# A key tile and a value tile of the self attention's latent made together in the two halves of TensorE's rows

## The chip, the cores and the metric

One core of a Trainium2 chip runs the whole kernel. The metric is the device time in microseconds (us) of one execution, as the median of several. The engines are TensorE (PE, with its weight loads as PEld), VectorE (DVE), ScalarE (ACT), GpSimd (POOL) and SyncE (SP), which issues most DMAs.

## The reference

Four sequences of 512 rows and 256 columns pass through two blocks: a cross attention on a context of 512 rows, and then a self attention whose keys and values come out of a latent of 64 columns each, followed by a gated layer of experts. Cut to what the change touches:

```python
q = (src @ Wq).reshape(Bb, Tt, H, DH).transpose(0, 2, 1, 3)
k = (src @ Wk_c @ Wk).reshape(Bb, Tt, H, DH).transpose(0, 2, 1, 3)   # latent 64, then 256
v = (src @ Wv_c @ Wv).reshape(Bb, Tt, H, DH).transpose(0, 2, 1, 3)   # latent 64, then 256
q = _apply_rope(q, sin, cos)
k = _apply_rope(k, sin, cos)
attn = jnp.einsum('bhqd,bhkd->bhqk', q, k) / np.sqrt(DH).astype(np.float32)
attn = jax.nn.softmax(attn, axis=-1)
sa = jnp.einsum('bhqk,bhkd->bhqd', attn, v)
```

## The kernel before

The attentions are eight instances, n = 0 to 7: four cross attentions (kind "c"), then four self attentions (kind "s"). Each has 16 heads in four quarters (groups) of four heads, and a quarter has 16 steps s, one for each of 4 key tiles and 4 heads, so that an instance has 64 steps. In each step TensorE makes the scores of one unit (L1695, 98 x 512, bf16) and ACT takes their exponential (L909). In each odd step TensorE also makes two more score tiles for the row maxima of a later quarter, 12 pairs ahead (max_pair, L1637), and DVE reduces the pair (row_max, L1156). In each fourth step comes the product of four probability tiles with the values (values, L1665: four heads side by side, 128 x 512 in f32, two passes each). At step 8 of a quarter the last quarter's heads are turned (L1651), at step AT_MAX its maxima (L1644); the turned maxima go by ACT (L802) and a DMA (L807) into the query stack.

While instance n runs, its successor m = n + 1 is prepared in stage tiles, that the lists CROSS_STEPS and SELF_STEPS put at steps of n (a negative step lies in n - 1). FA_STEPS does the same for the output projection of the last self attention. "tile" is TensorE's work, "empty" the copy of that tile out of its bank by DVE or ACT (OWNER). Of a self attention tiles 0 and 1 are transposes, 2 and 3 the two halves (even, odd) of the queries, 4 the latent (both halves of 64 in one tile cT), 5 and 6 the two halves of the keys (L1566: rows 0 to 63 of TensorE, 512 columns, f32) and 7 and 8 the values (L1571: rows 64 to 127, twice 256 columns). DVE empties tiles 2, 3, 5 and 6 by rotating them (L1088 to L1094, two instructions each), ACT the values (L856). Then "sum" adds the two products of a rotation on POOL (L651), "part0" and "part1" are copies to bf16 on ACT (L829, L833), "rest" and "part2" differences on POOL (L656, L661). Each part is written to scratch by SP (L525, L531) and read back as the stacks of the next instance (L546, L560), of which the first quarter is needed by the pair at step 41.

Scores, turned maxima and stage tiles share three banks in turn: the order of PE's work gives each its slot, and one may start when the work three slots earlier has been emptied. TensorE's order is fixed, so a tile that waits for its slot holds up all that follows. Row maxima have two double banks of their own, in which turned heads also take a place.

The four lines that matter most:

```python
                    f = t - 5
                    last = MM(o, fkv[0:DC, f * P:(f + 1) * P], cT[0:DC, 0, :], start=True, stop=True)
...
                        last = MM(o[:, j * D:(j + 1) * D], cT[DC:2 * DC, 0, tt * P:(tt + 1) * P], fkv[DC:2 * DC, :],
                                  start=True, stop=True)
```

Of the kernel before, what the change touches and what calls it, by code (L numbers as in the profile page):

```python
# [14 lines left out]
P = 128  # L15
HG = 4
# [5 lines left out]
LEAD = 12  # L22
FILL = 24
PROB_SLOTS = 3
AT_COPY, AT_HEADS, AT_MAX, AT_ROWS = 4, 8, 9, 11
SCORE_BANKS = [0, 1, 7]
END_BANKS = [0, 1, 7, 6, 2, 3, 4, 5]

# [7 lines left out]
def flamingo_block(nc, x, ctx_in, g_xattn, g_ffn, wq, bq, wk, bk, wv, bv,  # L36
                   f_wq, f_wkc, f_wvc, f_wk, f_wv, f_wo, f_in, f_out, f_w1, f_w2,
                   f_gg, f_ge, f_gb, f_eb, n1, n2, rope, out):
    B, L, D = x.shape
# [17 lines left out]
    DC = f_wkc.shape[1]  # L57
# [13 lines left out]
    INST = [("c", 0), ("c", 1), ("c", 2), ("c", 3), ("s", 0), ("s", 1), ("s", 2), ("s", 3)]  # L71
# [13 lines left out]
    def hook(n, step, *what):  # L85
        a = n * UNITS + step
        HOOKS.setdefault((a // UNITS, a // STEPS % NG, a % STEPS), []).append(what)

    CROSS_STEPS = [("stats", 0, -34), ("norm", 1, -20), ("norm", 0, -16), ("tile", 2, -12), ("empty", 2, -12), ("tile", 0, -11),
        ("empty", 0, -11), ("tile", 3, -10), ("empty", 3, -10), ("tile", 1, -6), ("empty", 1, -6), ("tile", 4, -5),  # L90
        ("empty", 4, -5), ("tile", 5, -5), ("empty", 5, -5), ("tile", 6, -4), ("empty", 6, -4), ("part0", 0, -3),
        ("part1", 0, 1), ("rest", 0, 1), ("empty", 8, 2), ("tile", 8, 2), ("part2", 0, 2), ("tile", 7, 3),
        ("empty", 7, 3), ("part0", 1, 3), ("rest", 1, 4), ("tile", 9, 5), ("empty", 9, 5), ("part1", 1, 7),
        ("part2", 1, 10)]
    SELF_STEPS = [("stats", 0, -28), ("norm", 0, -21), ("norm", 1, -20), ("tile", 0, -14), ("empty", 0, -14), ("tile", 1, -9),
        ("empty", 1, -8), ("tile", 4, -4), ("empty", 2, -3), ("empty", 4, -3), ("tile", 2, -3), ("tile", 3, -2),
        ("empty", 3, -2), ("tile", 5, -1), ("empty", 5, 0), ("sum", 0, 1), ("tile", 6, 2), ("empty", 6, 2),
        ("sum", 1, 2), ("tile", 7, 5), ("empty", 7, 5), ("part0", 0, 5), ("rest", 0, 5), ("tile", 8, 7),
        ("empty", 8, 7), ("rest", 1, 8), ("part2", 1, 8), ("part0", 1, 10), ("part1", 0, 14), ("part2", 0, 14),
        ("part1", 1, 16)]  # L100
    FA_STEPS = [("fatile", 0, 12), ("faempty", 0, 12), ("faempty", 1, 15), ("fatile", 1, 15), ("faempty", 2, 19), ("fatile", 2, 19),
        ("fatile", 3, 23), ("faempty", 3, 23), ("fastats", 0, 32), ("nf", 0, 43)]

    SELF_NO = {m: sum(k_ == "s" for k_, _ in INST[:m + 1]) for m in range(NI)}
    for n in range(1, NI):
        m = n + 1
        if m < NI:
            for what, i, step in (CROSS_STEPS if INST[m][0] == "c" else SELF_STEPS):
                hook(n, step, what, m, i)
        if INST[n - 1][0] == "s":  # L110
            for what, i, step in FA_STEPS:
                hook(n, step, what, INST[n - 1][1], i)


    BEGIN = [[2, 3, 6, 7, 0, 1, 4, 5, 8, 9], [2, 3, 6, 7, 8, 0, 1, 4, 5, 9]]

    def kind_of(stage, m):
        return "fa" if stage == "fa" else "b" if m == 0 else INST[m][0]
# [5 lines left out]
    SLOTS = []  # L124

    for m_ in range(2):
        SLOTS.extend(("proj", m_, t_) for t_ in BEGIN[m_])
    SLOTS.append(("turned", 0))
    for u_ in range(NI * UNITS):
        n_, g_, s_ = u_ // UNITS, u_ // STEPS % NG, u_ % STEPS  # L130
        SLOTS.append(("unit", u_))
        if s_ == AT_MAX and u_ // STEPS + 1 < GROUPS:
            SLOTS.append(("turned", u_ // STEPS + 1))
        for what_, m_, i_ in HOOKS.get((n_, g_, s_), []):
            if what_ in ("tile", "fatile"):
                SLOTS.append(("proj" if what_ == "tile" else "fa", m_, i_))
    STAGE = [key for key in SLOTS if key[0] in ("proj", "fa")]
    SLOTS = [key for key in SLOTS if key not in ASIDE]
    SLOT = {key: k for k, key in enumerate(SLOTS)}

    FILLED, EMPTIED, done = {}, {}, {"A": 0, "V": 0}
    EMPTYING = [("proj", m_, t_) for m_ in range(2) for t_ in BEGIN[m_]]
    for a_ in range(NI * UNITS):
# [2 lines left out]
                        if what_ in ("empty", "faempty"))  # L146
    for key in STAGE:
        FILLED[key] = len(FILLED) + 1
    for key in EMPTYING:
        who = OWNER[kind_of(key[0], key[1])][key[2]]  # L150
        done[who] += 1
        EMPTIED[key] = (who, done[who])
# [77 lines left out]
    with es:  # L230
# [9 lines left out]
        fkv = sb("fkv", [P, D], F32)  # L240
# [34 lines left out]
        cT = sb("cT", [P, CT, L], F32)  # L275
# [92 lines left out]
        s_tf = sem("stage_tile_full")  # L368
# [414 lines left out]
        def _(act):  # L783
# [94 lines left out]
            def begin_second():  # L878
                for t in BEGIN[1][:4] + BEGIN[1][5:9]:
                    if t == 6:  # L880
# [589 lines left out]
        def _(pe):  # L1470
            MM, TR = nc.tensor.matmul, nc.tensor.transpose
# [11 lines left out]
            def emptied(key):  # L1483

                if key[0] == "unit":
                    pe.wait_ge(s_exp, key[1] + 1)
                elif key[0] == "turned":
                    pe.wait_ge(s_mts, key[1] + 1)
                else:
                    who, count = EMPTIED[key]  # L1490
                    if count > waited[who]:
                        waited[who] = count
                        pe.wait_ge(s_ta if who == "A" else s_tv, count)

            def take(key):
                if key in ASIDE:
                    return slot_bank(key)
                k = slots[0]
                slots[0] += 1
                assert SLOTS[k] == key  # L1500
                if k >= 3:
                    emptied(SLOTS[k - 3])
                return slot_bank(key)
# [43 lines left out]
            def self_tile(m, t):  # L1547
                b = INST[m][1]
                o = take(("proj", m, t))
                if t < CT:  # L1550
                    if t == 0:
                        pe.wait_ge(s_set, 1)
                        pe.wait_ge(s_w, 16 * N_LARGE)
                        pe.wait_ge(s_src, 2 * (m + 1))
                    last = turn(o, src[b], t)
                elif t < 4:
                    emptied(("proj", m, 1))
                    f = t - 2
                    last = product(o, [(fq[:, c, f * P:(f + 1) * P], nT[:, c, :]) for c in range(CT)])
                elif t == 4:  # L1560
                    emptied(("proj", m, 1))
                    last = product(o, [(fkvc[:, c, :], nT[:, c, :]) for c in range(CT)])
                elif t < 7:
                    emptied(("proj", m, 4))
                    f = t - 5
                    last = MM(o, fkv[0:DC, f * P:(f + 1) * P], cT[0:DC, 0, :], start=True, stop=True)  # L1566
                else:
                    emptied(("proj", m, 4))
                    for j in range(2):
                        tt = 2 * (t - 7) + j  # L1570
                        last = MM(o[:, j * D:(j + 1) * D], cT[DC:2 * DC, 0, tt * P:(tt + 1) * P], fkv[DC:2 * DC, :],  # L1571
                                  start=True, stop=True)
                last.then_inc(s_tf, 1)

            def begin():
# [4 lines left out]
                pe.wait_ge(s_id, 4)  # L1580
                for t in BEGIN[0]:
                    if t == 6:
# [4 lines left out]
                    cross_tile(0, t)  # L1587
                for t in BEGIN[1][:5]:
                    cross_tile(1, t)
# [97 lines left out]
            for n in range(NI):  # L1687
                for g in range(NG):
                    gi = n * NG + g
                    for s in range(STEPS):  # L1690
                        u = gi * STEPS + s
                        kt, h = divmod(s, HG)
                        if s == 0:
                            pe.wait_ge(s_mrow, (gi + 1) * 16)
                        MM(take(("unit", u)), ks[:, g, h, kt * P:(kt + 1) * P], qs[:, g, h, :],  # L1695
                           start=True, stop=True).then_inc(s_sT, 1)
                        if u == 0:
                            max_pair(LEAD - 1)
                        q = u // 2 + LEAD
                        if s % 2 and q < N_PAIRS:  # L1700
                            max_pair(q)
                        if h == HG - 1 and (kt or gi):
                            values(*((gi, kt - 1) if kt else (gi - 1, TT - 1)))
                        if s == AT_HEADS and gi > 0:
                            turn_heads(gi - 1)
                        if s == AT_MAX and gi + 1 < GROUPS:
                            turn_max(gi + 1)
                        for what, m, i in HOOKS.get((n, g, s), []):
                            if what == "tile":
                                (cross_tile if INST[m][0] == "c" else self_tile)(m, i)  # L1710
                            elif what == "fatile":
                                self_output(m, i)
# [177 lines left out]
```

## Time and profile before

| what | value |
|---|---|
| median of 3 executions | 781.66 us (779.74 to 782.42) |
| the profiled execution | 780.02 us |
| its span, first to last instruction | 778.2 us |
| mean granted TensorE clock | 0.993 |
| busy: PE, DVE, ACT, POOL | 743.0, 514.7, 408.5, 217.9 us |

The steps of the eight instances take the span from 50 to 525 us; what follows is the layer of experts. The profile's busy time of PE counts matmuls with modelled ends. Times below are us from the start of the span. A row of the timeline has the start, the duration, the engine, the line, the operation, out<-in, the shapes and a count, and in brackets the idle time of the engine before it with what ended it; instructions that follow each other are merged into one row.

### The profile page before, as it was taken

To read this page: it belongs to the slowest core of one execution; us is meant where nothing else is said; L and a number is where in the kernel's file an instruction comes from. 1 tells how busy PE (TensorE), PEld (TensorE's weight loads), DVE (VectorE), ACT (ScalarE), POOL (GpSimd) and SP (SyncE) were. 2 spreads that over 40 slices of the span, in tenths; PEclk is the share of its full clock that TensorE was granted. 3 is DMA by queue.
4 is the path that set the end of the run, shared out by engine and by line. 5 is a ranking of instruction groups with operands and counts; after the bars stand their busy time and mean duration, and the time that the engine had idled before them with its cause. 6 is when DMAs were issued, how large, how long until landed. Compare 5 with 4: busy or idle time off the path is not lost.

```text
span 778.2 us, 10386 instructions
## 1 busy us (share of the span) xinstructions
PE 743.0 (95%) x3534; PEld 342.0 (44%) x3534; DVE 514.7 (66%) x777; ACT 408.5 (52%) x767; POOL 217.9 (28%) x326
## 2 busy tenths in 40 slices
PE   8879999999999999999999999999999999999995
PEld 5422343243233233233423432424644766458884
DVE  5679848847978878878797788762457222532765
ACT  4356867777767776875774867675211221222000
POOL 5232133223315415303321510010103721400444
PEclk9999999999999999999999999999999999999998
DMA  8783233315215414512421232006001564000011
GB/s 266 203 241 79 59 108 125 82 47 193 61 51 165 125 42 123 150 41 83 126 80 41 96 110 83 1 2 217 0 1 74 203 202 153 24 1 1 28 41 41
DMA packets 51892, 73.31 MB, mean 94 GB/s; under 512 B 7808, under 2 KB 42880, under 8 KB 51840
## 3 DMA queue, kind: packets, MB, share of 16 engines
q1 hardware_dynamic: 47248, 63.80, 28.1%
q0 software_dynamic: 2816, 8.46, 2.9%
q8 instruction: 29, 0.48, 0.3%
q10 hardware_dynamic: 1776, 0.40, 0.3%
q14 instruction: 23, 0.19, 0.1%
HBM read 45.04 MB, written 27.33 MB: 93 GB/s over the span
## 4 chain that ended last, share of the span: by engine, by line
PE 71%; DVE 14%; ACT 5%; issue 3%; DMA 3%; POOL 2%; SPq 0%; POOLq 0%; DVEq 0%; ACTq 0%
PE ps L1512 31%; PE ps L1665 12%; PE ps L1695 12%; PE ps L1637 11%; DVE negm L1156 7%; ACT hS L909 3%; PE ps L1507 2%; POOL scrf L744 2%; DVE bst L1034 2%; PE ps L1571 1%; PE ps L1651 1%; DMA rows<-in_L_xattn_wq_dram 1%; DMA w<-mTs 1%; DMA scrq<-mix 1%; PE ps L1566 1%
## 5 line engine op out<-in xcount | busy, mean ns | idle before, releaser
L1156 DVE TENSOR_REDUCE negm<-ps 128x2 f32<-128x1024 f32 x256 | 303.5, 1220 | 72.0 <-PE ps L1637 64.4
L909 ACT ACTIVATE hS<-ps 128x512 f32<-128x512 f32 x512 | 280.7, 604 | 116.6 <-PE ps L1695 114.7
L1695 PE MATMUL ps<-w 98*128 98x512 bf16 x512 | 170.1, 385 | 9.5 <-DMA w<-mTs 4.7
L1637 PE MATMUL ps<-w 96*128 96x512 bf16 x512 | 154.4, 383 | 7.8 <-DVE negm L1156 4.4
L1665 PE MATMUL ps<-hS,mix 128*17 128x512 f32 x1024 | 134.7, 598 | 0.2
L1695 PEld LDWEIGHTS ps<-w 98*128 98x128 bf16 x512 | 43.8, 97 | 161.5 <-ACT hS L909 76.6
L1637 PEld LDWEIGHTS ps<-w 96*128 96x128 bf16 x512 | 47.8, 98 | 60.4 <-DVE negm L1156 10.8
L1356 DVE SCALAR_TENSOR_TENSOR ctxs<-qk,ps 128x512 f32<-128x512 f32 x32 | 22.0, 687 | 72.0 <-ACT qk L945 71.0
L945 ACT ACTIVATE qk<-ps 128x512 f32<-128x512 f32 x32 | 19.1, 597 | 81.6 <-PE ps L1512 81.6
L1512 PE MATMUL ps<-w,hS 128*128 x256 | 55.6, 379 | 0.0
L1512 PEld LDWEIGHTS ps<-w,hS 128*128 128x128 f32 x256 | 48.6, 190 | 7.0 <-issue 0.5
L656 POOL TENSOR_TENSOR qk<-qk,mix 128x1024 f32<-128x1024 f32 x14 | 29.8, 2129 | 50.9 <-ACT mix L829 50.6
L633 POOL TENSOR_TENSOR mdif<-bst 128x4 f32<-128x4 f32 x12 | 2.5, 206 | 146.5 <-DVEq L996 146.5
L1665 PEld LDWEIGHTS ps<-hS,mix 128*17 128x17 f32 x1024 | 17.0, 95 | 53.9 <-ACT hS L909 29.4
L671 POOL TENSOR_SCALAR hS<-hS,tg 128x256 f32<-128x256 f32 x16 | 14.9, 930 | 92.0 <-DVEq L1182 92.0
L651 POOL TENSOR_TENSOR qk<-qk,hT 128x1024 f32<-128x1024 f32 x8 | 18.8, 2351 | 76.1 <-DVEq L996 76.1
L661 POOL TENSOR_TENSOR mix<-qk,mix 128x1024 bf16<-128x1024 f32 x14 | 29.9, 2133 | 26.6 <-ACT mix L833 25.5
L1512 PE MATMUL ps<-cT,fin 128*128 128x512 f32 x64 | 28.6, 595 | 0.3 <-ACT cT L938 0.3
L744 POOL DMA_INDIRECT scrf<-rows,place x16 | 15.7, 978 | 47.1 <-DVEq L996 42.5
L1359 DVE SCALAR_TENSOR_TENSOR hS<-ctxs,ps 128x512 f32<-128x512 f32 x32 | 22.0, 687 | 10.0 <-PE ps L1512 9.7
L1512 PE MATMUL ps<-rope_sb,fin 128*128 128x512 f32 x64 | 28.2, 594 | 0.0
L1512 PE MATMUL ps<-wT,fin 128*128 128x512 f32 x64 | 28.1, 592 | 0.0
(211 smaller groups left out, 867.3 us busy)
## 6 DMA issues: line engine op xcount, KB each, us to landing
w<-scrq SPq DMA_DIRECT2D x32, 384.0 KB, 4.1
scrk<-mix SPq DMA_DIRECT2D x24, 256.0 KB, 2.2
scrq<-mix SPq DMA_DIRECT2D x16, 384.0 KB, 3.3
scrq<-mix SPq DMA_DIRECT2D x24, 256.0 KB, 2.5
w<-scrk SPq DMA_DIRECT2D x32, 192.0 KB, 2.9
w<-scrk SPq DMA_DIRECT2D x32, 128.0 KB, 2.9
w<-in_L_ffn_W_experts_dram SPq DMA_DIRECT2D x8, 512.0 KB, 8.1
mix<-scrf SPq DMA_DIRECT2D x4, 528.0 KB, 3.9
```

Of the source, the lines that this page charges most:

```text
L656: link(pool.tensor_tensor(qk[X][:], qk[X][:], parts[X][:, 0], ALU.subtract))
L661: link(pool.tensor_tensor(parts[X][:, 2], qk[X][:], parts[X][:, 1], ALU.subtract))
L744: pool.indirect_dma_start(dst[:], bass.IndirectOffsetOnAxis(ap=place[:, tile:tile + 1], axis=0), source, None).then_inc(done, 16)
L909: nc.scalar.activation(prob[:, kt % PROB_SLOTS, s % HG, :], slot_bank(("unit", u)), ACT.Exp, scale=SC).then_inc(s_exp, 1)
L945: nc.scalar.activation(th[k % 4], end_full(f"{name}{b}", 2 * p), ACT.Tanh, scale=0.5).then_inc(s_th, 1)
L1156: V.tensor_reduce(negm[:, gi % 2, h, 2 * t2:2 * t2 + 2], ps[:, bank:bank + 2, :], AX.X, ALU.max, negate=True).then_inc(s_re, 1)
L1356: V.scalar_tensor_tensor(out=uu[:, k % 2, :], in0=th[k % 4], scalar=1.0, in1=end_full(f"{name}{b}", 2 * p), op0=ALU.add, op1=ALU.mult).the ...
L1359: V.scalar_tensor_tensor(out=hS[:, b * TT:(b + 1) * TT, p, :], in0=uu[:, k % 2, :].rearrange("p (t j) -> p t j", t=TT), scalar=0.5, in1=en ...
L1512: last = MM(o, w, r, start=(j == 0), stop=(j == len(terms) - 1))
L1637: last = MM(ps[:, bank + t, :], qs[0:STK, g, h, tt * P:(tt + 1) * P], ks[0:STK, g, h, :], start=True, stop=True)
L1665: last = MM(ps[32 * h:32 * h + VM, 6, :], vp[n % 2][:, kt, g * HG + h, :], prob[:, kk % PROB_SLOTS, h, :], start=(kt == 0), stop=(kt == TT ...
L1695: MM(take(("unit", u)), ks[:, g, h, kt * P:(kt + 1) * P], qs[:, g, h, :], start=True, stop=True).then_inc(s_sT, 1)
```

## The change

A value tile is made in the same step as a key tile: 7 with 5, and 8 with 6. Each of the two takes a slot, the key tile the first; the key matmul uses rows 0 to 63 of TensorE, the two value matmuls rows 64 to 127. Who empties a key tile waits for both tiles. The steps of many pieces are different: of a self attention's preparation tile 5 goes from step -1 to 3, tile 6 from 2 to 4, tiles 7 and 8 from 5 and 7 to 3 and 4, both sums from 1 and 2 to 5 and 6, part0 from 5 and 10 to 9 and 13, part1 from 14 and 16 to 17 and 19, the rests from 5 and 8 to 9 and 11, part2 from 14 and 8 to 13 and 11, and tile 0 from -14 to -17. Of a cross attention's preparation tile 3 goes from -10 to -8, tile 8 from 2 to 5, and a rest from 4 to 2. The output projection's third tile goes from 19 to 18. AT_MAX goes from 9 to 10. `h == 3` is the same as `h == HG - 1`.

```diff
-AT_COPY, AT_HEADS, AT_MAX, AT_ROWS = 4, 8, 9, 11
+AT_COPY, AT_HEADS, AT_MAX, AT_ROWS = 4, 8, 10, 11
...
-    CROSS_STEPS = [("stats", 0, -34), ("norm", 1, -20), ("norm", 0, -16), ("tile", 2, -12), ("empty", 2, -12), ("tile", 0, -11),
-        ("empty", 0, -11), ("tile", 3, -10), ("empty", 3, -10), ("tile", 1, -6), ("empty", 1, -6), ("tile", 4, -5),
-        ("empty", 4, -5), ("tile", 5, -5), ("empty", 5, -5), ("tile", 6, -4), ("empty", 6, -4), ("part0", 0, -3),
-        ("part1", 0, 1), ("rest", 0, 1), ("empty", 8, 2), ("tile", 8, 2), ("part2", 0, 2), ("tile", 7, 3),
-        ("empty", 7, 3), ("part0", 1, 3), ("rest", 1, 4), ("tile", 9, 5), ("empty", 9, 5), ("part1", 1, 7),
-        ("part2", 1, 10)]
-    SELF_STEPS = [("stats", 0, -28), ("norm", 0, -21), ("norm", 1, -20), ("tile", 0, -14), ("empty", 0, -14), ("tile", 1, -9),
-        ("empty", 1, -8), ("tile", 4, -4), ("empty", 2, -3), ("empty", 4, -3), ("tile", 2, -3), ("tile", 3, -2),
-        ("empty", 3, -2), ("tile", 5, -1), ("empty", 5, 0), ("sum", 0, 1), ("tile", 6, 2), ("empty", 6, 2),
-        ("sum", 1, 2), ("tile", 7, 5), ("empty", 7, 5), ("part0", 0, 5), ("rest", 0, 5), ("tile", 8, 7),
-        ("empty", 8, 7), ("rest", 1, 8), ("part2", 1, 8), ("part0", 1, 10), ("part1", 0, 14), ("part2", 0, 14),
-        ("part1", 1, 16)]
+    CROSS_STEPS = [("stats", 0, -34), ("norm", 1, -20), ("norm", 0, -16), ("tile", 2, -12), ("empty", 2, -12), ("tile", 0, -11), ("empty", 0, -11), ("tile", 3, -8), ("empty", 3, -8), ("tile", 1, -6), ("empty", 1, -6), ("tile", 4, -5), ("empty", 4, -5), ("tile", 5, -5), ("empty", 5, -5), ("tile", 6, -4), ("empty", 6, -4), ("part0", 0, -3), ("part1", 0, 1), ("rest", 0, 1), ("part2", 0, 2), ("rest", 1, 2), ("tile", 7, 3), ("empty", 7, 3), ("part0", 1, 3), ("empty", 8, 5), ("tile", 8, 5), ("tile", 9, 5), ("empty", 9, 5), ("part1", 1, 7), ("part2", 1, 10)]
+    SELF_STEPS = [("stats", 0, -28), ("norm", 0, -21), ("norm", 1, -20), ("tile", 0, -17), ("empty", 0, -17), ("tile", 1, -9), ("empty", 1, -8), ("tile", 4, -4), ("empty", 2, -3), ("empty", 4, -3), ("tile", 2, -3), ("tile", 3, -2), ("empty", 3, -2), ("tile", 5, 3), ("empty", 7, 3), ("empty", 5, 4), ("tile", 6, 4), ("empty", 6, 4), ("empty", 8, 4), ("sum", 0, 5), ("sum", 1, 6), ("part0", 0, 9), ("rest", 0, 9), ("rest", 1, 11), ("part2", 1, 11), ("part0", 1, 13), ("part2", 0, 13), ("part1", 0, 17), ("part1", 1, 19)]
...
+    BESIDE = {5: 7, 6: 8}
+
+    def made(what, m, t):
+
+        both = what == "tile" and INST[m][0] == "s" and t in BESIDE
+        return [("proj" if what == "tile" else "fa", m, t_) for t_ in ([t, BESIDE[t]] if both else [t])]
...
-                SLOTS.append(("proj" if what_ == "tile" else "fa", m_, i_))
+                SLOTS.extend(made(what_, m_, i_))
...
+    for stage_, m_, t_ in STAGE:
+        if stage_ == "proj" and INST[m_][0] == "s" and t_ in BESIDE:
+
+            FILLED[stage_, m_, t_] = FILLED[stage_, m_, BESIDE[t_]]
...
-                elif t < 7:
+                else:
+
+                    f = t - 5
+                    values_ = take(("proj", m, BESIDE[t]))
                     emptied(("proj", m, 4))
-                    f = t - 5
-                    last = MM(o, fkv[0:DC, f * P:(f + 1) * P], cT[0:DC, 0, :], start=True, stop=True)
-                else:
-                    emptied(("proj", m, 4))
+                    MM(o, fkv[0:DC, f * P:(f + 1) * P], cT[0:DC, 0, :], start=True, stop=True).then_inc(s_tf, 1)
                     for j in range(2):
-                        tt = 2 * (t - 7) + j
-                        last = MM(o[:, j * D:(j + 1) * D], cT[DC:2 * DC, 0, tt * P:(tt + 1) * P], fkv[DC:2 * DC, :],
+                        tt = 2 * f + j
+                        last = MM(values_[:, j * D:(j + 1) * D], cT[DC:2 * DC, 0, tt * P:(tt + 1) * P], fkv[DC:2 * DC, :],
                                   start=True, stop=True)
                 last.then_inc(s_tf, 1)
```

## Rows read from the trace of the kernel before

**Rows 1.** The page: busy us of an engine, share of the span, instructions.

```profile
PE 743.0 (95%) x3534; PEld 342.0 (44%) x3534; DVE 514.7 (66%) x777; ACT 408.5 (52%) x767; POOL 217.9 (28%) x326
```

**Rows 2.** By stretch: length, busy of PE, PEld, DVE, ACT, POOL; PEclk, DMA.

```profile
234.16:250.44 16.28, 15.69 (x81) 5.22 (x80) 14.05 (x17) 12.49 (x23) 9.56 (x6) 1.00 0.47 157
250.44:262.58 12.14, 12.14 (x73) 3.60 (x70) 10.52 (x13) 10.40 (x21) 5.92 (x4) 1.00 0.34 111
...
422.89:440.13 17.24, 16.66 (x88) 6.18 (x88) 14.59 (x17) 13.46 (x24) 7.84 (x4) 1.00 0.28 87
```

**Rows 3.** Timeline of PE, end of instance 2 to step 8 of instance 3.

```profile
232.13 1.05 PE L1665 MATMUL ps<-hS,mix 128*17 128x512 f32 x8
233.11 1.12 PE L1566 MATMUL ps<-cT,fkv 64*128 64x512 f32 x2
234.16 0.61 PE L1695 MATMUL ps<-w 98*128 98x512 bf16 x2
...
235.69 0.39 PE L1695 MATMUL ps<-w 98*128 98x512 bf16 x1 [0.48 <-DVE qk L1089]
236.01 1.12 PE L1566 MATMUL ps<-cT,fkv 64*128 64x512 f32 x2
...
239.77 1.13 PE L1571 MATMUL ps<-fkv,cT 64*128 64x256 f32 x4
240.83 0.60 PE L1695 MATMUL ps<-w 98*128 98x512 bf16 x2
...
243.84 0.39 PE L1695 MATMUL ps<-w 98*128 98x512 bf16 x1
```

**Rows 4.** Timeline of DVE, the same stretch: row maximum, then rotations of tiles 5 and 6.

```profile
233.04 1.23 DVE L1156 TENSOR_REDUCE negm<-ps 128x2 f32<-128x1024 f32 x1 [0.18 <-DVE hT L1094]
234.34 0.69 DVE L1088 TENSOR_TENSOR qk<-ps,rope_sb 128x512 f32<-128x512 f32 x1
234.95 0.68 DVE L1089 TENSOR_TENSOR qk<-ps,rope_sb 128x512 f32<-128x512 f32 x1
...
237.17 0.69 DVE L1092 SCALAR_TENSOR_TENSOR hT<-ps,rope_sb 128x512 f32<-128x512 f32 x1 [0.41 <-PE ps L1566]
```

**Rows 5.** Who PE waited for from 234.16 to 481: total us, times, longest.

```profile
PE ps L1695 <- DVE qk L1089: 1.9, 4, 0.5
```

**Rows 6.** Timeline of ACT in instance 3: parts and exponentials.

```profile
251.39 1.09 ACT L833 ACTIVATE mix<-qk 128x1024 bf16<-128x1024 f32 x1
252.34 2.09 ACT L909 ACTIVATE hS<-ps 128x512 f32<-128x512 f32 x4
```

**Rows 7.** Timeline of POOL in instance 3: a rest behind the heads, the last part.

```profile
247.91 2.13 POOL L656 TENSOR_TENSOR qk<-qk,mix 128x1024 f32<-128x1024 f32 x1 [0.18 <-POOL rows L672]
...
254.87 2.14 POOL L661 TENSOR_TENSOR mix<-qk,mix 128x1024 bf16<-128x1024 f32 x1 [0.18 <-POOL mix L661]
```

**Rows 8.** Timeline of SP: the next first quarter's query stack is read.

```profile
263.05 0.42 SPq L560 DMA_DIRECT2D w<-scrq  x1
```

**Rows 9.** The page's DMA issues: KB each, median us to landing.

```profile
w<-scrq SPq DMA_DIRECT2D x32, 384.0 KB, 4.1
```

**Rows 10.** Timeline of PE: the pair at step 41 of instance 3.

```profile
269.97 0.59 PE L1637 MATMUL ps<-w 96*128 96x512 bf16 x2 [0.28 <-DVE negm L1156]
```

**Rows 11.** Timeline, all engines, steps 2 to 7 of instance 1: a cross preparation.

```profile
109.97 1.99 PE L1512 MATMUL ps<-wT,cT 128*128 128x256 f32 x8
...
113.67 0.76 DVE L1073 TENSOR_TENSOR mix<-ps,bv_bc 128x256 f32<-128x256 f32 x2 [2.55 <-PE ps L1665]
...
115.55 0.69 ACT L843 ACTIVATE qk<-ps,bqk 128x512 f32<-128x512 f32 x1 [2.71 <-PE ps L1512]
...
118.12 0.38 PE L1695 MATMUL ps<-w 98*128 98x512 bf16 x1
...
118.84 0.39 PE L1695 MATMUL ps<-w 98*128 98x512 bf16 x1 [0.34 <-ACT hS L909]
```

More of the change, by code:

```diff
@@ L101, in flamingo_block @@
-    FA_STEPS = [("fatile", 0, 12), ("faempty", 0, 12), ("faempty", 1, 15), ("fatile", 1, 15), ("faempty", 2, 19), ("fatile", 2, 19),
-        ("fatile", 3, 23), ("faempty", 3, 23), ("fastats", 0, 32), ("nf", 0, 43)]
+    CROSS_STEPS = [("stats", 0, -34), ("norm", 1, -20), ("norm", 0, -16), ("tile", 2, -12), ("empty", 2, -12), ("tile", 0, -11), ("empty", 0, -11), ("tile", 3, -8), ("empty", 3, -8), ("tile", 1, -6), ("empty", 1, -6), ("tile", 4, -5), ("empty", 4, -5), ("tile", 5, -5), ("empty", 5, -5), ("tile", 6, -4), ("empty", 6, -4), ("part0", 0, -3), ("part1", 0, 1), ("rest", 0, 1), ("part2", 0, 2), ("rest", 1, 2), ("tile", 7, 3), ("empty", 7, 3), ("part0", 1, 3), ("empty", 8, 5), ("tile", 8, 5), ("tile", 9, 5), ("empty", 9, 5), ("part1", 1, 7), ("part2", 1, 10)]
@@ L104, in flamingo_block @@
+    FA_STEPS = [("faempty", 0, 12), ("fatile", 0, 12), ("fatile", 1, 15), ("faempty", 1, 15), ("faempty", 2, 18), ("fatile", 2, 18), ("fatile", 3, 23), ("faempty", 3, 23), ("fastats", 0, 32), ("nf", 0, 43)]
     SELF_NO = {m: sum(k_ == "s" for k_, _ in INST[:m + 1]) for m in range(NI)}
@@ L1701, in _ @@
                             max_pair(q)
-                        if h == HG - 1 and (kt or gi):
+                        if h == 3 and (kt or gi):
                             values(*((gi, kt - 1) if kt else (gi - 1, TT - 1)))
```

## The prediction

> **What bounds the kernel now.** I read the page's busy table first: PE has 95% [rows 1]. The stretches say where that holds: in the first two quarters of instance 3, where the change works, PE is busy 15.69 of 16.28 and 12.14 of 12.14 us, DVE 14.05 and 10.52, ACT 12.49 and 10.40 [rows 2]. So PE sets the time, but DVE and ACT have so little room that an idle PE is soon theirs: this is a kernel in which PE's order, not its sum, has to be walked. The granted clock is 1.00 in all of them, so no term for it. Then PE's timeline: a key tile takes 1.05 us from its start to the next score (233.11 to 234.16, 236.01 to about 237.06), a value tile 1.06 (239.77 to 240.83) [rows 3]. Last, who PE waits for: four times in four instances, 0.5 us each, a score for the rotation on DVE [rows 5]; by start to start the wait before 235.69 is 0.65 (two scores of 0.22 and a pair of 0.44 after 234.16 end at 235.04) [rows 3].
>
> **Part 1, two tiles at once.** Four self attentions are prepared, two double tiles each: eight. If the value passes run beside the key passes, a value tile's 1.06 us vanishes: 8 x 1.06 = 8.5 us gross. No row shows two row halves at work together. The bounds: at the least only the change of the array's shape between the two is saved, about 0.2 (1.05 less two passes of 512 f32 columns at 0.43); at the most 1.06. A double tile that costs more than two single ones is excluded, since the same passes are issued. Nearest is the value product: its eight f32 passes of 512 columns, four heads in four column strips, take 0.98 us up to the next work (232.13 to 233.11), as long as the two passes of one tile [rows 3]. So I take the upper end, 1.05 for a double tile.
>
> A rule speaks against this. In that row two passes of each of four heads end in the time of two, though the code issues head after head; a queue in which each pass starts only after the one before it in the program would need five starts 0.43 apart, over 2.1 us [rows 3]. The Trainium skill, TensorE: Matmul & The Clock Gate, Part 3, holds that matmuls start and end strictly in program order, without reordering. By that rule and head-wise order the key's second pass would hold back the first value pass. Its result is rival A.
>
> **Part 2, the new waits of the first quarter.** I walk instance 3 on the clock of the profiled execution, with the steps' new order [rows 3, 4]. Up to the value product of step -1, at 233.11, nothing differs. Tile 5 no longer follows, so units 0 and 1, their pair, units 2 and 3 and their pair run through to 234.85; the value product ends with the shape change at 235.93. Double tile (5, 7): 235.93 to 236.99. Unit 4 ends at 237.2. Now double tile (6, 8) needs the slot of tile 5, three places back. DVE has done its three row maxima (1.2 each from 233.04) by 236.7, so it isn't late; it starts 1.16 after the tile's start, as with tile 6 before (236.01 to 237.17), and rotates for 1.29 (234.34 to 235.63) [rows 4]: 237.09 to 238.38. PE starts 0.06 later, at 238.44, idle for 1.2. Queued behind this wait is all of TensorE: unit 5, the pair of step 5, the next values; ACT gets no scores meanwhile. Double tile (6, 8) to 239.49, unit 5 and a pair to 240.15. Unit 6 has the slot of tile 6, rotated 239.60 to 240.89: 240.95, idle 0.8. Unit 7, pair and values bring unit 8 to 242.90, against 243.84 before [rows 3]. So two tiles saved (2.1) and one old wait gone (0.65) pay for 2.0 of new waits.
>
> From unit 8 to the quarter's end the kernel before took 6.6 (243.84 to 250.44) [rows 2, 3]. By the queue's work (eight scores, four pairs, two value products, turned heads) it is 6.1, and ACT's copy of part0, now at steps 9 and 13 instead of 5 and 10, lets it come to 6.3. The quarter ends at 249.2, 1.2 us earlier.
>
> **Part 3, the copies that come later.** ACT's parts of 1.06 us [rows 6] were at steps 5, 10, 14 and 16; they come to lie at 9, 13, 17 and 19. Chained exponentials cost 0.48 each ((2.09 less 0.66) / 3), a part 0.95 (251.39 to 252.34) [rows 6]. In the second quarter: part1 at step 17 starts at 250.6, exponentials 18 and 19 follow at 251.6 and 252.1, part1 at 19 at 252.6, exponential 20 at 253.5 to 254.1. Unit 23 needs that slot; PE would be there at 253.2 and starts at 254.16: 1.0 us idle. Before, with the part at 16, four exponentials ran through [rows 6]. So instances 3 and 4 keep 1.2 - 1.0 = 0.2 to 0.3 us each. In 5 and 6 the output projection puts four more tiles between steps 12 and 23 (the first quarter takes 17.24 instead of 16.28 [rows 2]); the same walk gives 1.3 for the first quarter and 0.1 of wait at step 23, since PE arrives later: 1.3 each once their small waits are in. Sum: 2 x 0.3 + 2 x 1.3 = 3.2 us.
>
> **Part 4, POOL, SP and the stacks.** POOL has no steps of its own: its sums come as early as before, and the order of a rest and the heads (steps 5 and 8, now 8 and 9) swaps, at no cost, as heads go ahead of the next rest already [rows 7]. The rests and third parts hang on ACT's parts, so the last third part ends some 1.2 us after 257.0 (254.87 + 2.14) [rows 7], and SP's writes to scratch and its read of the next stack move by as much. That query stack was issued at 263.05 [rows 8] with a median of 4.1 us to landing [rows 9], and the pair at step 41 that needs it started at 269.97, then waiting for DVE [rows 10]. Of 2.8 us of room 1.2 goes; behind a slow transfer PE loses between 0 and 1.2 in one instance. I put 0.4 on it.
>
> **Part 5, the cross pieces.** In instances 1 and 2, tile 8 leaves step 2, where it cost 1.8 us of PE (109.97 on) before a DVE that sat 2.55 us idle for it, its row maxima behind [rows 11]. In step 5 it comes after tile 7. Tile 7's copy on ACT, which waited 2.71 us for PE [rows 11], starts 1.9 us earlier, the part and the exponentials after it too. Unit 7 at 118.84 started 0.5 after unit 6 had ended (118.12 + 0.22), waiting for ACT [rows 11]; walked anew it starts at 118.0. Gain 0.8 each, bounds 0 and 0.8: 1.6 us. Tile 3 at -8 moves one wait of 0.3 from one unit to another: nothing. Tile 0 at -17 and AT_MAX at 10 keep the waits they have (the turned maximum still has a step before its DMA at 11); I take a loss of 0.2 for tile 0's later copies on ACT. The rest at 2 instead of 4 has nothing between on POOL. The third output tile one step earlier: nothing.
>
> **The sum.** 3.2 + 1.6 - 0.4 - 0.2 = 4.2 us. The profiled execution took 780.02: 775.8 by its own time. That is 1.6 below the median of 781.66, so on the median's scale 777.5 us.
>
> **The rivals.** A: passes leave in program order. Each of eight double tiles costs 0.43 more, and its rotation waits for the values too: 3.4 us, leaving 0.8: 780.9. Against it stands the value product [rows 3]; for it, that column strips needn't behave as row halves. B, the slower side: the two halves don't overlap at all. Then a double tile takes 1.05 + 0.85, and DVE, that waits for both tiles, starts 0.85 later; twice in each instance, both on the chain through the waits of part 2: 4 x 1.7 = 6.8, so 2.6 slower: 784.3. It decides from an overlap of about 0.3 of the value tile's 0.85 downwards (8 x 0.53 = 4.2). C: the banks become the bound. Two tiles hold two of three slots, ACT's waits at step 23 come in all four instances (2 more), and the cross gain is hidden by ACT (1.6): 0.6 faster, 781.1. For it: ACT has 10.40 of 12.14 in the second quarter before the parts arrive there [rows 2]. D: waits of part 2 are smaller, because DVE's rotation overlaps with PE's pair, and the stall at 23 doesn't come: 4 us more, 773.5.
>
> **How the numbers follow.** Forecast 0.52 (774.5 to 780), A 0.09, B 0.12, C 0.19, D 0.08. Differences under 0.3%, 2.3 us, can't be told from none in this kernel. Faster are D and most of the forecast, 0.57; the same A, C and the forecast's upper edge, 0.30; slower B and a little of C with a late stack, 0.13. The range goes from 773.5 (D) to 783.0, between C and B, which leaves out most of B and the tail below D.
>
> **What would show it.** Right: in the first quarter of instance 3 the rows of L1566's key and value passes start together and the next score comes 1.05 us later; PE idle twice for DVE, 1.2 and 0.8, at units 4 to 6; the wait before unit 2 gone; a wait for ACT near step 23 in instances 3 and 4 and none in 5 and 6; unit 7 of instance 1 without its wait; the quarter 1.2 us shorter. Wrong: a double tile of 1.3 (A) or 1.9 (B); PE waiting for the stack at step 41 in more than one instance; waits for DVE over 1.5.

## The result and the profile after

The changed kernel takes 782.96 us (median of 22 executions, 780.39 to 784.38) against 781.67 us of the kernel before (22 executions on the same chips): ratio 1.0016, 95% interval 1.0009 to 1.0023. It is 1.3 us slower. The interval does not reach 1, but the difference is smaller than the 0.3% that the prediction took as the least that can be told; 0.5% faster was forecast. The 782.96 lies inside the range, 0.04 below its upper end. The ratios here and below leave out executions far slower than the others of their kernel, such as one of 857.88 us in e_parts.

The page of after (busy us, share of the span, instructions) answers to [rows 1], the stretches answer to [rows 2]: the first and second quarter of instance 3, from score to score of their step 0.

```profile
PE 736.6 (94%) x3534; PEld 341.3 (44%) x3534; DVE 514.1 (66%) x777; ACT 408.9 (52%) x767; POOL 217.5 (28%) x326
```
```profile
231.41:248.03 16.62, 14.60 (x86) 5.08 (x82) 13.85 (x17) 11.79 (x22) 8.65 (x6) 1.00 0.49 154
248.03:262.50 14.47, 12.30 (x70) 3.53 (x70) 11.92 (x13) 11.43 (x21) 7.89 (x5) 1.00 0.44 138
```

PE is busy for 6.4 us less in all, so the two halves do work at once; but the second quarter, 12.14 before with PE busy throughout, takes 14.47 with 12.30 busy. The timeline of PE from the end of instance 2, which answers to [rows 3]:

```profile
233.25 1.05 PE L1667 MATMUL ps<-hS,mix 128*17 128x512 f32 x8
234.23 0.69 PE L1570 MATMUL ps<-cT,fkv 64*128 64x512 f32 x1
234.24 0.70 PE L1573 MATMUL ps<-fkv,cT 64*128 64x256 f32 x2
234.76 0.59 PE L1570 MATMUL ps<-cT,fkv 64*128 64x512 f32 x1
234.77 0.59 PE L1573 MATMUL ps<-fkv,cT 64*128 64x256 f32 x2
235.29 0.39 PE L1697 MATMUL ps<-w 98*128 98x512 bf16 x1
236.87 0.69 PE L1570 MATMUL ps<-cT,fkv 64*128 64x512 f32 x1 [1.18 <-DVE qk L1091]
...
237.93 0.39 PE L1697 MATMUL ps<-w 98*128 98x512 bf16 x1
...
239.43 0.60 PE L1697 MATMUL ps<-w 98*128 98x512 bf16 x2 [0.68 <-DVE hT L1096]
```

Key and value passes start 0.01 us apart, and the next score comes 1.06 us after the key tile's start, as after one tile alone. Then PE waits twice for the rotations. Waits are counted here by the scores' rate: what follows a score starts 0.22 us after it, what follows a pair 0.44, so that all beyond it is a wait. The two are 1.36 us (235.29 + 0.22 to 236.87) and 0.84 (a score of 0.22 and a pair of 0.44 after 237.93, to 239.43). All of this is as forecast. What was not forecast stands in the next rows: PE from the end of the first quarter on, then DVE, then POOL.

```profile
248.03 0.61 PE L1697 MATMUL ps<-w 98*128 98x512 bf16 x2 [0.16 <-DMA w<-mTs]
...
251.72 0.38 PE L1697 MATMUL ps<-w 98*128 98x512 bf16 x1
252.94 0.39 PE L1697 MATMUL ps<-w 98*128 98x512 bf16 x1 [0.84 <-ACT hS L911]
...
256.00 0.38 PE L1697 MATMUL ps<-w 98*128 98x512 bf16 x1
257.28 0.23 PE L1646 MATMUL ps<-identb,m 128*128 128x128 bf16 x1 [0.90 <-DVEq L998]
257.34 0.38 PE L1697 MATMUL ps<-w 98*128 98x512 bf16 x1
258.16 0.60 PE L1639 MATMUL ps<-w 96*128 96x512 bf16 x2 [0.43 <-DVE hS L1180]
```
```profile
255.06 1.89 DVE L1166 CAST m<-negm 128x16 bf16<-128x16 f32 x1
256.99 0.18 DVE L1167 TENSOR_TENSOR m<-negm,m 128x16 bf16<-128x16 f32 x1
257.38 0.26 DVE L1179 RECIPROCAL rec<-ps 128x16 f32<-128x16 f32 x1 [0.22 <-DVE m L1167]
257.67 0.42 DVE L1180 TENSOR_TENSOR hS<-ps,rec 128x256 f32<-128x256 f32 x1
```
```profile
254.79 2.13 POOL L663 TENSOR_TENSOR mix<-qk,mix 128x1024 bf16<-128x1024 f32 x1 [0.18 <-POOL mix L663]
```

The wait at step 23 is the forecast one: 1.00 (251.72 + 0.22 to 252.94). Then a cast of 16 numbers per partition on DVE, which elsewhere takes 0.17 us, takes 1.89. It ends at 256.95, and POOL's third part, which had begun 0.27 before it, ends at 256.92. TensorE's turning of the maxima waits for the cast and the difference behind it: 1.06 (256.00 + 0.22 to 257.28), and the next pair waits for the heads that DVE scales still later: 0.60. Instance 4 has the same rows. In 5 and 6 the cast takes 1.31, and PE does not wait for it.

The same collision stood in the kernel before, one quarter earlier, with POOL's rest instead of its third part. And in the second quarter the same cast already met the end of the same third part, which ran there till 257.01 (254.87 + 2.14 [rows 7]): 0.24 us instead of 0.17, to 257.03. The rows of before are DVE, then POOL, then the turned maxima on PE:

```profile
243.16 1.60 DVE L1164 CAST m<-negm 128x16 bf16<-128x16 f32 x1
...
256.79 0.24 DVE L1164 CAST m<-negm 128x16 bf16<-128x16 f32 x1
```
```profile
242.61 2.13 POOL L656 TENSOR_TENSOR qk<-qk,mix 128x1024 f32<-128x1024 f32 x1 [1.64 <-ACT mix L829]
```

```profile
245.16 0.22 PE L1644 MATMUL ps<-identb,m 128*128 128x128 bf16 x1
```

The collision of the first quarter cost nothing there: value tile 8, a score, the heads, a score and a pair kept PE busy from 242.78 to 245.16, and the cast had ended at 244.76.

**Lengths of quarters**, from timelines, score of step 0 to score of step 0, in us. Each is read from one profiled execution. A quarter that the edits leave alone agrees from run to run to about 0.05, but for the first two of instance 0 (14.31 to 15.56 and 11.93 to 12.94); the time ahead of the first score (47.3 to 49.6) and behind the last (248.4 to 251.1) varies by more than the effects here, in no order that follows the kernels. So mechanisms are read from the quarters, and verdicts from the medians.

| quarter | before | after | e_short | e_max9 | e_parts | e_spread | e_best |
|---|---|---|---|---|---|---|---|
| instance 1, first (2 the same) | 18.06 | 17.45 | 17.45 | 17.45 | 18.05 | 17.45 | 17.45 |
| instance 0, fourth (1 the same) | 19.96 | 20.18 | 20.18 | 20.17 | 19.96 | 20.17 | 19.96 |
| instance 2, third and fourth | 32.46 | 31.70 | 31.70 | 31.57 | 32.46 | 31.40 | 31.41 |
| instance 3, first | 16.27 | 16.62 | 16.63 | 16.27 | 16.28 | 16.27 | 16.27 |
| instance 3, second | 12.14 | 14.47 | 12.95 | 16.18 | 14.54 | 12.79 | 12.01 |
| instance 4, second | 12.08 | 14.40 | 12.95 | 14.46 | 14.46 | 12.71 | 12.01 |
| instance 5, third and fourth | 33.47 | 32.69 | 32.40 | 32.65 | 33.87 | 32.82 | 32.82 |

### The profile page after: what moved, and what is told of

Read it like the earlier page. It is cut to its first block, busy times and chain, and to the rows that moved or that the text cites. A ratio compares the mean times of both kernels' runs of the same rounds, so it can differ in the third digit from the quotient of the medians.

```text
span 780.8 us, 10394 instructions
## 1 busy us (share of the span) xinstructions
PE 736.6 (94%) x3534; PEld 341.3 (44%) x3534; DVE 514.1 (66%) x777; ACT 408.9 (52%) x767; POOL 217.5 (28%) x326
## 4 chain that ended last, share of the span: by engine, by line
PE 73%; DVE 13%; ACT 6%; issue 4%; DMA 3%; POOL 0%; SPq 0%; POOLq 0%; DVEq 0%; ACTq 0%
PE ps L1514 35%; PE ps L1667 12%; PE ps L1697 11%; PE ps L1639 10%; DVE negm L1158 6%; ACT hS L911 4%; PE ps L1509 2%; DVE bst L1036 2%; PE ps L1653 1%; DMA w<-mTs 1%; DMA rows<-in_L_xattn_wq_dram 1%; PE ps L1570 1%; DVE m L1166 1%; PE ps L1573 1%; DMA scrq<-mix 0%
## 5 line engine op out<-in xcount | busy, mean ns | idle before, releaser
L1514 PE MATMUL ps<-fout,hS 128*128 128x256 f32 x128 | 30.0, 392 | 2.7 <-issue 2.7
L1514 PEld LDWEIGHTS ps<-fout,hS 128*128 128x128 f32 x128 | 25.2, 198 | 7.6 <-issue 4.2
```

The lines of the kernel that those rows point to most:

```text
L1514: last = MM(o, w, r, start=(j == 0), stop=(j == len(terms) - 1))
```

## The experiments

The theory: the double tiles give what was forecast, and two things take it back: the third part on POOL holds DVE's cast where PE waits for it (1.06 and 0.60 in each of instances 3 and 4), and moved pieces bring smaller waits. The rivals: the double tiles' new waits are themselves the price; the moved copies on ACT cost it without POOL; the cross pieces lose it.

**The cross pieces alone** (e_cross: the kernel before with the new CROSS_STEPS).

> The kernel before with the change's steps of the cross preparation alone (tile 8 at 5, tile 3 at -8, a rest at 2). Theory: this part of the change works as forecast; the first quarters of instances 1 and 2 go from 18.06 to about 17.45 us each, as in the changed kernel, and the whole gains 1.2 us (ratio 0.9985). Rival: ACT hides it and the shorter quarters of the changed kernel come from its other parts; ratio 1.000.

Measured: 779.87 us, before 780.54, ratio 0.9995 (0.9982 to 1.0009). The first quarter of instance 1, 18.06 before:

```profile
107.79:125.24 17.45, 17.45 (x93) 7.41 (x90) 11.91 (x17) 13.23 (x24) 9.96 (x6) 1.00 0.64 193
```

The cross pieces give 0.61 in each of instances 1 and 2, and the fourth quarters ahead of them take back 0.22 each: 0.78 in all. They are not where the loss is. (The whole, 0.4 us less with an interval that holds 1, could not tell.)

**POOL's third parts cut short** (e_short: after, with the third parts of the self attentions made for 16 of 512 columns; the rest of them is left out).

```diff
-                link(pool.tensor_tensor(parts[X][:, 2], qk[X][:], parts[X][:, 1], ALU.subtract))
+                n_ = 16 if INST[m][0] == "s" else L
+                link(pool.tensor_tensor(parts[X][:, 2, :, 0:n_], qk[X][:, :, 0:n_], parts[X][:, 1, :, 0:n_], ALU.subtract))
```

> The changed kernel, in which POOL's third parts of the self attentions are left out but for 16 of each 512 columns (the rest of their third part is stale). Collision theory: the third parts hold up VectorE's cast of the row maxima; without them the casts of the second quarters of instances 3 and 4 fall from 1.89 to about 0.18 us, TensorE's waits at steps 26 and 27 (1.06 and 0.6) shrink to 0.2 in sum, the quarter goes from 14.47 to about 13.0 us, and the whole gains about 3 us on the changed kernel. Copies theory: the loss there comes from ACT's two copies at steps 17 and 19, which put everything behind; quarter about 14.4 us, no gain.

Measured: 779.49 us, ratio to before 0.9985 (0.9973 to 0.9996), where after stands at 1.0016. DVE in instance 3, and the second quarter:

```profile
257.14 0.17 DVE L1167 CAST m<-negm 128x16 bf16<-128x16 f32 x1
```
```profile
250.11:263.06 12.95, 12.11 (x70) 3.62 (x70) 10.19 (x13) 11.22 (x21) 4.10 (x5) 1.00 0.54 159
```

With nothing taken from ACT, PE or DVE, the cast is back at 0.17, and the second quarter is shorter by 1.52 (instance 4: 1.45). The wait for ACT at step 23 stays. This shows the cause: the length of POOL's operation sets the length of the cast beside it. The two quarters together are 3.0 us shorter; the two ratios differ by 0.0031, 2.4 us, with intervals of some 0.001 each.

**POOL's operations in halves** (e_split: after, with each of its sums, rests and third parts as two instructions of 512 columns; the edit of the third part is shown).

```diff
-                link(pool.tensor_tensor(parts[X][:, 2], qk[X][:], parts[X][:, 1], ALU.subtract))
+                pool.tensor_tensor(parts[X][:, 2, 0], qk[X][:, 0], parts[X][:, 1, 0], ALU.subtract).then_inc(s_pool, 1)
+                k[0] += 1
+                link(pool.tensor_tensor(parts[X][:, 2, 1], qk[X][:, 1], parts[X][:, 1, 1], ALU.subtract))
```

> The changed kernel with each of POOL's sums, rests and third parts made as two instructions of half the columns. Collision theory: what holds up the cast is one POOL instruction, so the cast waits for a half (1.07 us) at most: 1.89 falls to below 1.0, the second quarters of instances 3 and 4 from 14.47 to about 13.6 us, the whole gains 1.5 to 2 us on the changed kernel. Copies theory, or a cast that is slowed by POOL's work as such and not by an instruction: cast and quarter as they are, no gain.

Measured: 782.67 us, ratio 1.0033 (1.002 to 1.0047), the second quarter of instance 3 14.55: nothing gained. DVE, then POOL:

```profile
255.33 1.06 DVE L1172 CAST m<-negm 128x16 bf16<-128x16 f32 x1
256.42 1.08 DVE L1173 TENSOR_TENSOR m<-negm,m 128x16 bf16<-128x16 f32 x1
```
```profile
255.20 1.15 POOL L667 TENSOR_TENSOR mix<-qk,mix 128x512 bf16<-128x512 f32 x1 [0.18 <-POOL mix L669]
256.31 1.16 POOL L669 TENSOR_TENSOR mix<-qk,mix 128x512 bf16<-128x512 f32 x1
```

The cast gets in when the first half ends (255.33 + 1.06 = 256.39, the half at 256.35). By then the second half has begun, and it holds DVE's next operation, the difference, till 257.50. PE needs both, so it waits as long as before. The expectation missed this: two short holds in a row are as long as one.

The Trainium skill, SBUF — State Buffer, section SBUF: two separate sides, says that VectorE and GpSimd share a pair of ports which the one that starts first keeps for its whole instruction, the other being blocked, and that among VectorE's operations those with two operands in SBUF and those in a two-port mode are concerned. The rows agree as far as they go: both DVE operations read SBUF alone and end 0.03 to 0.04 us after the POOL operation that they met, while a row maximum, which reads the banks, keeps 1.23 under a third part (in after from 253.80, the third part from 252.47). That the cast runs in such a mode no row shows. And by the profile, whose spans on POOL are rough, not every POOL operation holds the cast for its whole time: under one of 128 x 4 numbers it takes 0.17 in after, and ends 0.4 before it (POOL, then DVE):

```profile
206.57 1.04 POOL L646 TENSOR_TENSOR scale<-nvar,mhalf 128x4 f32<-128x4 f32 x1
```
```profile
206.99 0.17 DVE L1166 CAST m<-negm 128x16 bf16<-128x16 f32 x1
```

**AT_MAX back at 9** (e_max9: after, with that one number).

> The changed kernel with AT_MAX back at 9. Theory of the late maximum: TensorE's wait of 0.33 us for the row of maxima at step 16 of instances 3 and 4 comes from turning them a step later; it goes, and the whole gains 0.6 us. Rival: the DMA of the maxima waits for the scratch writes of part0, which now go just ahead of it (step 9 instead of 5); the wait stays near 0.33 and nothing is gained.

Measured: 781.22 us, ratio 1.0008 (0.9997 to 1.002). The first quarters lose their wait for w<-mTs: 16.62 to 16.27 (instances 3 and 4), 17.36 to 17.24 (5 and 6), and the third quarters of instances 2 to 4 go from 13.55 to 13.41. So AT_MAX at 10 costs some 1.4 us in all, against nothing in the prediction. The collision stays (cast 1.88), and PE now waits 1.27 in one piece. In instance 3 something else comes on top; the stretches of its second quarter, the third column from the end being the granted clock:

```profile
247.99:258.85 10.86, 8.70 (x53) 2.77 (x53) 8.73 (x10) 9.36 (x18) 6.96 (x5) 1.00 0.39 128
258.85:262.27 3.42, 3.42 (x13) 0.70 (x6) 1.77 (x2) 1.10 (x3) 1.07 (x2) 0.50 0.55 162
```

After PE's waits at steps 23 and 25 the clock falls to 0.50 (1.2 instead of 2.4 GHz) for 3.42 us, and the quarter takes 16.18 where instance 4, with the same waits and a clock of 1.00, takes 14.46.

**The moved pieces without double tiles** (e_parts: the kernel before, tiles and all else as they were, with the new steps of the sums, parts and rests of a self attention).

> The kernel before, all tiles at their old steps and single, with the change's steps of the sums, copies, rests and third parts alone. Collision and copies theories together: the loss comes with the pieces' new steps and not with the double tiles. The casts of the second quarters of instances 3 and 4 take 1.5 us or more (0.24 before), TensorE waits 1.0 for ACT near step 23, the quarter goes from 12.1 to about 14 us, the first quarter's long cast (1.60) goes; the whole is about 3 us slower than before. Rival: the loss needs the double tiles, whose waits put the cast where POOL works; then quarters and time stay as before.

Measured: 786.11 us, before 780.22, ratio 1.0068 (1.0048 to 1.0087): 5.3 us slower by the ratio. The second quarter of instance 3, and PE in it:

```profile
249.04:263.58 14.54, 12.37 (x73) 3.53 (x70) 12.26 (x13) 11.45 (x22) 7.74 (x5) 1.00 0.43 138
```
```profile
254.03 0.39 PE L1690 MATMUL ps<-w 98*128 98x512 bf16 x1 [0.84 <-ACT hS L904]
```

Without a double tile the second quarter has the same length as after's, with the same wait of 1.0 at step 23 and the held cast (1.88). So the loss of the second quarters belongs to the later copies and third parts, and the rival that the double tiles' waits are the price falls. Over the four preparations of self attentions e_parts takes 4.8 us more than before, and after, with the same places of these pieces and its other moves, 2.0 more: by this comparison the double tiles give something even there.

**One half after the other** (e_serial: after, with TensorE waiting for the key matmul's end before the value matmuls).

```diff
+                    pe.wait_ge(s_tf, FILLED["proj", m, BESIDE[t]] - 1)
                     for j in range(2):
```

> The changed kernel, in which TensorE waits for the end of the key tile before it starts the value tile, so that nothing overlaps. If the overlap is what saves the tile, the double tile goes from 1.06 to 2.1 us or a little more (0.85 of matmuls and the way of a semaphore), each of two a quarter puts the rotation and all behind it as much later, the first quarters of instances 3 to 6 take 2.0 to 2.4 us more (16.62 to about 18.8, 17.36 to about 19.5). If the quarter is bound by VectorE or ACT instead, it takes less than 1 us more.

Measured, one execution: 802.36 us. PE at the first double tile, then two stretches of the first quarter:

```profile
234.26 1.12 PE L1570 MATMUL ps<-cT,fkv 64*128 64x512 f32 x2
235.44 1.13 PE L1574 MATMUL ps<-fkv,cT 64*128 64x256 f32 x4
236.50 0.39 PE L1698 MATMUL ps<-w 98*128 98x512 bf16 x1
```
```profile
231.44:239.79 8.35, 7.10 (x32) 2.71 (x29) 4.72 (x5) 3.64 (x7) 2.35 (x1) 1.00 0.68 212
239.79:246.62 6.83, 6.83 (x22) 1.74 (x21) 4.09 (x6) 2.48 (x5) 2.35 (x1) 0.50 0.00 0
```

In series the double tile takes 2.24 against 1.06 (1.18 for the key tile, 1.06 for the value tile), so the overlap is the whole value tile, as the prediction took it. The quarter is 4.8 longer, not the 2.0 to 2.4 that two such tiles and their rotations would give: for 6.83 us the granted clock was 0.50.

**Pieces back near their old steps** (e_spread: after with its double tiles, but sums at 1 and 6, part0 at 3 and 9, part1 at 5 and 14, rests at 3 and 9, part2 at 10 and 14, tile 0 at -14, AT_MAX 9).

> The changed kernel with its double tiles at steps 3 and 4, AT_MAX at 9, tile 0 at -14, and the copies and POOL's pieces spread so that no third part runs when VectorE casts: part0 at 3 and 9, part1 at 5 and 14, rests at 3 and 9, third parts at 10 and 14. Collision and copies theory: the casts take 0.18 us in both quarters, the waits at steps 16, 23 and 26 go, the first two quarters of instances 3 and 4 take about 16.3 and 12.1 to 12.4 us, and the whole is about 6 us faster than the changed kernel, 4 to 5 faster than before (ratio 0.994). Rival: the waits for the rotation (1.36 and 0.84) let ACT and POOL fall behind in any order, and new waits of 1 to 2 us come up in the second quarter; ratio 0.998 to 1.000.

Measured: 775.51 us, before 780.22, ratio 0.9942 (0.9929 to 0.9955). No cast takes over 0.25 us in instances 3 to 6. The second quarter, and what is left in it, PE and ACT:

```profile
247.62:260.40 12.78, 12.34 (x73) 3.57 (x69) 10.54 (x13) 10.28 (x20) 5.79 (x4) 1.00 0.44 130
```
```profile
249.00 0.88 PE L1697 MATMUL ps<-w 98*128 98x512 bf16 x2 [0.34 <-ACT hS L911]
```
```profile
247.40 1.06 ACT L835 ACTIVATE mix<-qk 128x1024 bf16<-128x1024 f32 x1 [0.60 <-POOLq L659]
```

Here part1 stood at the head of ACT's queue 0.60 us before POOL's rest was done, with the exponentials of the next steps behind it, and PE waited for these 0.50 and 0.27.

**Double tiles further apart** (e_two_six: e_spread with double tiles at steps 2 and 6, POOL's second sum held back until the cast is done, and the later pieces two to four steps later).

> As the run before, but the double tiles at steps 2 and 6, so that a pair and a value product (which need no slot) lie between a double tile and the unit that needs its slot; POOL's second sum waits for the cast. Theory of the slots: the waits of 1.36 and 0.84 for the rotation go, smaller waits for ACT (0.3 to 0.6 each, three of them) come; the first quarters take about 15.6 us, the whole is 7 to 9 us faster than the changed kernel (ratio to before 0.991). Rival: DVE and ACT are so full that the wait only moves; first quarters 16.3 us as in the run before.

Measured: 783.81 us, ratio 1.0048 (1.0035 to 1.0062). PE's waits in the first quarter of instance 3 and at its end, then ACT and POOL at that end:

```profile
233.75 0.66 PE L1572 MATMUL ps<-cT,fkv 64*128 64x512 f32 x1 [0.40 <-ACT hS L913]
237.34 0.39 PE L1699 MATMUL ps<-w 98*128 98x512 bf16 x1 [0.40 <-ACT mix L860]
238.90 0.67 PE L1572 MATMUL ps<-cT,fkv 64*128 64x512 f32 x1 [0.52 <-ACT hS L913]
240.23 0.39 PE L1699 MATMUL ps<-w 98*128 98x512 bf16 x1 [0.20 <-ACT hS L913]
...
250.61 0.79 PE L1699 MATMUL ps<-w 98*128 98x512 bf16 x2 [2.09 <-ACT hS L913]
```
```profile
248.93 1.06 ACT L833 ACTIVATE mix<-qk 128x1024 bf16<-128x1024 f32 x1 [2.27 <-POOLq L656]
```
```profile
246.49 2.35 POOL L655 TENSOR_TENSOR qk<-qk,hT 128x1024 f32<-128x1024 f32 x1 [0.55 <-POOL rows L676]
```

The rotations' waits of 1.36 and 0.84 are gone, and four waits for ACT (0.56, 0.57, 0.68, 0.27 by the scores' rate) take their place: 2.1 for 2.2. The 2.15 at the quarter's end (250.61 less 247.47 and the 0.99 of the product) comes from the sum: it came late, part0 stood in ACT's queue before it, and the exponentials behind. It was not the cast that held the sum back, since cast and difference were done by 243.2; at step 8 the sum stands on POOL behind the addition of the heads (L676 in its row). The expected 7 to 9 us of gain did not come. So this run says nothing for or against steps 2 and 6 but that the wait moves.

**The best order found** (e_best: e_spread with part1 and part2 of the second half at step 17 instead of 14, and a cross attention's tile 3 back at -10).

> The kernel e_spread with two moves: in the self attentions part1 1 and part2 1 go from step 14 to step 17, and in the cross attentions tile 3 goes back from step -8 to -10. Theory (a piece costs when it stands at the head of its engine's queue before what it needs is there, or beside another engine that holds VectorE's operation): in e_spread part1 1 stood in ScalarE's queue at step 14 before GpSimd's rest was done, and TensorE waited 0.50 and 0.27 us at steps 18 and 19; three steps later it should not, so the second quarter of the instances 3 and 4 goes from 12.79 and 12.71 to about 12.0 to 12.1 (0.7 each), and the fourth quarter before each cross attention from 20.18 back to 19.96 (0.22 each, two of them): 1.8 in all, some 773.7 us where e_spread had 775.5, ratio about 0.992. Rival: part1 1 at step 17 is late for the transposed operands that are needed from unit 32, or ScalarE's work there takes the same time from the exponentials of the steps behind it: then the second quarter stays at 12.7 or the third is longer by as much, and the ratio stays at 0.994.

Measured: 773.26 us, before 780.0, ratio 0.992 (0.9902 to 0.9937): faster than both kernels. The second quarter of instance 3, and what PE waited for most from 229.83 to 476 us (total us, times, longest):

```profile
246.10:258.10 12.00, 12.00 (x73) 3.61 (x69) 10.44 (x13) 9.91 (x19) 5.79 (x4) 1.00 0.43 129
```
```profile
PE ps L1570 <- DVE qk L1091: 4.7, 4, 1.2
PE ps L1697 <- DVE hT L1096: 2.7, 4, 0.7
...
```

Both moves paid what their waits had been: 0.78 and 0.70 in the second quarters, 0.22 in each of two fourth quarters. PE is busy throughout the second quarter again, and ACT for 9.91 us of it. What remains above all is the two waits for the rotations in each of four preparations, as in after. This order with single tiles was not run, so how much of the gain is the double tiles' stays open.

## Why the prediction was wrong

Forecast and measured, as changes in us of the quarters that a preparation touches (for the one that ends in instance 3: the third and fourth quarter of instance 2, and the first two of 3):

| preparation that ends | forecast | after, measured | e_best, measured |
|---|---|---|---|
| in instances 3 and 4 (self), each | -0.3 | +1.9 | -1.2, -1.1 |
| in instance 5 (self) | -1.3 | -1.1 | -1.6 |
| in instance 6 (self) | -1.3 | -0.7 | -0.7 |
| in instances 1 and 2 (cross), each | -0.8 | -0.4 | -0.6 |
| stack and tile 0, all | +0.6 | in the lines above | |
| sum | -4.2 | +1.2 | -5.8 |

**Part 1, the two halves: right.** The double tile takes 1.06 (forecast 1.05), and e_serial shows that without overlap it takes 2.24. Rivals A and B fall. The value's first passes start ahead of the key's second (234.24 and 234.76), though the code issues the whole key product first. The Trainium skill, TensorE: Matmul & The Clock Gate, Part 3, says that matmuls start and end in program order. With whole products in that order, as rival A had it, the rows do not agree; they do not show in which order the single passes stood in the queue.

**Part 2, the new waits: right in kind and nearly in size.** 1.36 and 0.84 against 1.2 and 0.8, and the old wait is gone. The first quarter of after holds the work that before did from tile 5's start to that quarter's end, 17.33 (233.11 to 250.44 [rows 2, 3]). It was to take 1.2 less; it takes 16.62, 0.71 less. Of the 0.49 missing, 0.16 is the first wait and 0.33 are waits at the quarter's end for the turned maxima, which Part 5 had put at nothing and which AT_MAX at 9 takes away (e_max9).

**Part 3, the later copies: right.** A wait for ACT of 1.00 at step 23 in instances 3 and 4 (forecast 1.0), and none in 5 and 6. e_parts shows it as the copies' own, without double tiles.

**Part 4: the step that failed.** It says that POOL's rests and third parts "hang on ACT's parts", ends the last third part 1.2 us later, and asks only what the stack at step 41 loses by that. It never lays POOL's moved operation beside what DVE does there. Counted from the start of the second quarter, the third part came at 4.4 before (254.87 less 250.44 [rows 2, 7]) and comes at 6.8 in after (254.79 less 248.03), onto the cast of step 24, whose result PE turns two steps later. That costs 1.52 and 1.45 (e_short), 3.0 us in instances 3 and 4, and is the largest missing term: 3.0 of the 5.4 by which the sum is off. The trace of before held the warning twice, in the cast of 1.60 beside a rest and in the cast of 0.24 at the end of the third part; PE waited for neither, and neither was among the rows that the prediction reads. The prediction's own numbers put the two together: the third part 1.2 later runs from 256.1 to 258.2, and the cast (256.79, less 1.2 for the shorter quarter, plus 1.0 for step 23) comes at about 256.6. The stack at step 41 itself made no wait, so the 0.4 put on it was too much.

**Part 5: three sizes off.** AT_MAX at 10 was said to keep its waits; it costs some 1.4 (e_max9). The cross gain was 0.61 instead of 0.8: unit 7 comes right behind unit 6, as forecast (one row from 117.04 in after, against the two of [rows 11]), but unit 6 itself is only 0.09 earlier from the quarter's start, where the walk needs 0.3. Tile 3 at -8, put at nothing, costs 0.22 twice, and e_best takes it back by tile 3 at -10 alone. Tile 0 at -17: 31.57 in e_max9 against 31.40 in e_spread, about 0.17 in each of instances 2 to 4, 0.5 in all where the prediction took 0.2.

The terms add up: 3.0 (collision), 1.4 (AT_MAX), 0.8 (cross) and 0.3 (tile 0) less 0.4 (stack) are 5.1 of 5.4. That the rest lies in the longer first wait (0.16, four times) and other small gains is worked out, not tested.

**The rivals.** C asked for ACT's waits at step 23 in all four instances; they came in 3 and 4, as the forecast had it, and not in 5 and 6. D asked for smaller waits than the forecast; they were a little larger. What decided was none of the four: an engine off the path held an operation of another that was off the path too, and its result was due. The range held the time only at its edge, and by luck: its upper end came from rivals that did not happen.

## What to carry to other kernels

When an engine's operation is moved, lay it beside every engine that it may hold up there, not only beside its producers and consumers: in the trace of before, look for operations whose duration differs from their like (here 1.60 against 0.17 for one cast), even where nothing waits, and ask whether the change puts such a meeting where its result is due. A double-up that saves work on the bounding engine pays only if the pieces that hang on it keep to steps at which their inputs are ready and no queue stands behind them: kernels with the same double tiles were 1.3 us slower than before with one list of steps and 6.2 us faster (0.8% of 780.0) with another.

## What the runs showed of the hardware

A DVE cast of 0.17 us took up to 1.89 when it came up under a long POOL operation on SBUF, and ended 0.03 us behind it; a shorter POOL operation brought it back to 0.17 (e_short), and halving it moved the second half of the hold to the next DVE operation (1.06 and 1.08 in e_split).

Key and value matmuls in the two row halves overlap wholly: 1.06 us for both up to the next score, 1.05 for the key tile alone, 2.24 for both with a wait between them.

The granted clock fell to 0.50 behind idle stretches of PE: for 3.42 us in instance 3 of e_max9, after waits of 1.0 and 1.27, and for 6.83 us in e_serial. The same two waits in instance 4 of e_max9 and in instance 3 of e_parts left it at 1.00. What decides between them was not tested; in e_max9 the fall cost 1.72 us (16.18 against 14.46), more than either wait.
